# A two-layer recurrent block on one core: merged fp32r attention, paired output products, and experts routed through DRAM in 39 tiles

## The reference

```python
x = L0_attn_x                                  # [2, 1024, 256]
xn = layernorm(x)
q = rope(xn @ W_Q.T); k = rope(xn @ W_K.T); v = xn @ W_V.T   # 16 heads of 16, 8 key/value heads
s = softmax(q k^T / sqrt(256)) v  -> @ W_O.T
g = silu(swiglu(xn, lut[gate_idx], lut[up_idx], lut[down_idx]))      # inner width 688, 16-entry table
x = x + s * g
xn = layernorm(x)
s = time_mix(xn)        # layernorm again, w/k/v/r, state = (1-w) state + k v, y = r . state, @ Wout; 4 heads of 64
# experts: 8 of width 176, the best 2 of each token count; a shared one of width 352
combine = top-2 softmax weights, renormalised, zero for the other 6
out = silu(x @ shared_gate.T) * (x @ shared_up.T) @ shared_down.T
out = out + sum_e combine_e * (silu(x @ gate_e.T) * (x @ up_e.T)) @ down_e.T
x = x + s * silu(out)
```

## Time and profile before

| | us |
|---|---|
| median of 3 runs | 1142.14 (1138.51 to 1142.19) |
| profiled execution, first to last instruction | 1137.0 |
| outside that span (median less span) | 5.1 |

### The profile page before, as it was taken

One profiled execution on the slowest core, in us unless ns is written; L12 is line 12 of the kernel. 1 busy time (PEld: TensorE's weight loads), 2 busy tenths in 40 slices (PEclk: granted clock), 3 DMA queues, 4 the chain that ended last, 5 costly groups with the idle time before them and its releaser, 6 DMA issues. The chain is left out here.

```text
span 1137.0 us, 18228 instructions
## 1 busy us (share of the span) xinstructions
PE 1029.0 (91%) x7112; PEld 625.2 (55%) x7112; DVE 730.6 (64%) x993; ACT 489.1 (43%) x864; POOL 378.5 (33%) x304
## 2 busy tenths in 40 slices
PE   4869999999999999998999999846899999999997
PEld 3722333333333333322687878745756788888886
DVE  6889777778777877770376554499923574434433
ACT  1412666666556555656542244130621343332322
POOL 3231444346434543456011000296600042323232
PEclk9866999999999999999999999865599999999999
DMA  4580111111111111100200000230000111211211
GB/s 164 179 276 19 31 33 33 34 28 33 32 33 32 33 33 33 37 12 12 69 1 1 2 1 1 77 126 3 2 3 1 47 59 35 74 47 57 65 56 47
DMA packets 43606, 52.87 MB, mean 46 GB/s; under 512 B 14216, under 2 KB 30472, under 8 KB 43256
## 3 DMA queue, kind: packets, MB, share of 16 engines
q1 hardware_dynamic: 43104, 50.99, 14.4%
q10 hardware_dynamic: 416, 0.72, 0.2%
HBM read 37.53 MB, written 12.06 MB: 44 GB/s over the span
## 5 line engine op out<-in xcount | busy, mean ns | idle before, releaser
L626 DVE TENSOR_REDUCE row_max<-psum 128x1 f32<-128x1024 f32 x256 | 302.6, 1218 | 87.5 <-PE psum L679 87.4
L611 ACT ACTIVATE probs_t<-psum 128x512 f32<-128x512 f32 x512 | 267.1, 603 | 199.9 <-PE psum L693 199.9
L703 PE MATMUL psum<-probs_t,VS 128*32 128x512 f32 x1024 | 206.9, 604 | 17.5 <-ACT o_sb L494 17.5
L581 POOL TENSOR_TENSOR lut_sum<-lut_sum,lut_tmp 128x1072 f32<-128x1072 f32 x60 | 149.4, 2490 | 200.1 <-DVE lut_tmp L644 199.4
L679 PE MATMUL psum<-KS,QS 96*128 96x512 bf16 x512 | 164.6, 405 | 13.0 <-DVE row_max L626 8.9
L693 PE MATMUL psum<-QS,KS 99*128 99x512 bf16 x512 | 153.7, 381 | 3.2 <-ACT probs_t L611 3.2
L1858 POOL TENSOR_TENSOR m_h_f<-m_h_f,comb_b 128x512 f32<-128x512 f32 x44 | 71.5, 1625 | 234.0 <-DVE m_h_f L1936 234.0
L679 PEld LDWEIGHTS psum<-KS,QS 96*128 96x128 bf16 x512 | 39.0, 98 | 158.7 <-DVE row_max L626 114.6
L1936 DVE TENSOR_TENSOR m_h_f<-psum,m_silu 128x512 f32<-128x512 f32 x56 | 38.7, 691 | 124.9 <-ACT m_silu L1893 124.9
L693 PEld LDWEIGHTS psum<-QS,KS 99*128 99x128 bf16 x512 | 48.9, 97 | 99.9 <-ACT probs_t L611 49.9
L1893 ACT ACTIVATE m_silu<-psum 128x512 f32<-128x512 f32 x56 | 33.4, 597 | 154.7 <-PE psum L392 154.7
(11 more groups left out here) (228 smaller groups left out, 1729.4 us busy)
## 6 DMA issues: line engine op xcount, KB each, us to landing
QS<-q_rows SPq DMA_DIRECT2D x32, 192.0 KB
m_raw<-experts_w SPq DMA_DIRECT2D x2, 2688.0 KB, 13.0
comb_b<-comb_rows SPq DMA_DIRECT2D x16, 256.0 KB, 3.3
q_rows<-part SPq DMA_DIRECT2D x8, 384.0 KB, 3.1
KS<-k_rows SPq DMA_DIRECT2D x16, 192.0 KB
x_tok<-x SPq DMA_DIRECT2D x4, 512.0 KB, 7.9
q_rows<-part SPq DMA_DIRECT2D x8, 256.0 KB, 4.0
ctxT<-o_sb SPq DMA_DIRECT2D x64, 32.0 KB, 2.0
```

The costliest lines, as they stand in the source:

```text
L581: nc.gpsimd.tensor_tensor(wsum[:, cols], wsum[:, cols], wtmp[:, slot % 3, :], ALU.add).then_inc(lut_add, 1)
L611: nc.scalar.activation(pt[:, k % NPT, :], ring(k)[:], ACT.Exp, scale=float(E) ** -0.5).then_inc(p_ready, 1)
L626: nc.vector.tensor_reduce(mx[:, n % 2, i:i + 1], m.psum[:, 2 * (k % 2):2 * (k % 2) + 2, :], AX_XY, ALU.max).then_inc(max_done, 1)
L703: nc.tensor.matmul(OB[32 * j:32 * (j + 1), :], m.VS[:, bb * NTT + t, kv, :], pt[:, k % NPT, :], start=(t == 0), stop=(t == NTT - 1)).then_ ...
```

## The change

1. **Projections and attention become one block**; the semaphores of this front part are cleared after it, with a barrier. ACT now makes the normalised tiles (`scale`) in place of DVE, the parts are two (fp32r high and low) in place of three, so the DVE residue and the second ACT cut are gone, and the v projections of the last two token blocks stand among the first maxima.
2. **fp32r attention operands.** An operand is 48 rows (3 slots x 16), 50 with the maxima, held as fp32r. The two query heads of a group lie at rows 0 and 64. Each group's load is 768 KB (576 KB before), four groups are held (`NQK`), 26 maxima stand ahead of the first step. `place_max(0)` is issued ahead of the table-index loads.
3. **`output`** puts the two heads' A products side by side, then the two state products.
4. **Routing.** `route` runs two steps per slot, then 14 steps of `place` turn it into a row number for each token and choice, with counts made on PE (`count_tokens`). POOL scatters each token's row twice to `x_rows` in DRAM: 32 indirect DMAs of 128 rows. DVE waits for all of them before it takes `s_tok`.
5. **Experts.** Rows sorted by expert lie in 39 tiles of 128 rows; each is turned, goes through the one expert that its number (`tile_w`, loaded into a PE register) names, and is stored to `y_rows`. POOL gathers both results of each token (32 indirect DMAs), and DVE combines. On PE a place of the loop holds `gate_up` of tile i (6 matmuls of 352 columns), `turn_h` of i-1 (2 transposes), `down_r` of i-2 (6 matmuls of 256 columns) and `turn_x` of i+2 (2 transposes); ACT and DVE follow in the same order. SP loads tile j+1 behind the store of tile j-4. The shared expert (3 chunks) is dense over 4 blocks, the first before, three after the routed tiles.

The core of the diff:

```diff
@@ attention: PE
-    mm = nc.tensor.matmul(MX[k % 2][h][:], QS[n % 3][0:NROW, i * P:(i + 1) * P],
-                          KS[n % 3][0:NROW, h * BLK:(h + 1) * BLK], start=True, stop=True)
+    st, g = divmod(i, G)
+    mm = nc.tensor.matmul(MX[k % 2][h][:], QS[n % NQK][rows(g, NROW), st * P:(st + 1) * P],
+                          KS[n % NQK][rows(g, NROW), h * BLK:(h + 1) * BLK], start=True, stop=True)
...
-                    maxima_ahead(k)
+                    for h in range(2):
+                        maximum(k, h)
                     scores(n, t, 0)
+                    scores(n, t, 1)
                     if t >= 1:
                         weigh(n, t - 1)
                     elif n >= 1:
                         weigh(n - 1, NTT - 1)
-                    maxima_ahead(k + 1)
-                    for j in range(1, NJ):
-                        scores(n, t, j)
+                    scores(n, t, 2)
+                    scores(n, t, 3)
+                    for h in range(2):
+                        maximum(k + 1, h)
@@ time mix: POOL and DVE
+            pool.wait_ge(idx_done, NIDX)
+            for n in range(NT):
+                pool.wait_ge(m.xr_ready, n + 1)
+                for c in range(2):
+                    nc.gpsimd.indirect_dma_start(m.x_rows, bass.IndirectOffsetOnAxis(ap=m.slots[:, c, n:n + 1], axis=0),
+                                                 m.xr[:, n, :], None).then_inc(m.scat, 16)
...
+            dve.wait_ge(m.scat, 16 * 2 * NT)
             for n in range(0, NT, 2):
                 dve.wait_ge(so_ps, n // 2 + 1)
@@ experts: SP, the routed loop on PE, POOL
+            def load(j):
+                if j >= 4:
+
+                    sp.wait_ge(t1_ps, j - 3)
+                sp.dma_start(xs[:, j % 4, :], m.x_rows[j * P:(j + 1) * P, :]).then_inc(xs_in[j % 4], 16)
+
+            def store(j):
+                sp.wait_ge(yo_done, j + 1)
+                sp.dma_start(m.y_rows[j * P:(j + 1) * P, :], yo[:, j % 4, :]).then_inc(ys_out[j % 4], 16)
+
+            for j in range(NTL + 4):
+                if j < NTL:
+                    load(j)
+                if j >= 4:
+                    store(j - 4)
...
+            for i in range(-2, NTL + 2):
+                if 0 <= i < NTL:
+                    at_expert[i] = pe.value_load(m.tile_w[0:1, i:i + 1], min_val=0, max_val=(NE - 1) * EW)
+                    gate_up(i, at_expert[i])
+                if 0 <= i - 1 < NTL:
+                    turn_h(i - 1)
+                if 0 <= i - 2 < NTL:
+                    down_r(i - 2, at_expert[i - 2])
+                if 0 <= i + 2 < NTL:
+                    turn_x(i + 2)
...
+            for i in range(4):
+                pool.wait_ge(ys_out[i], 16 * len(range(i, NTL, 4)))
+            for tb in range(NB):
+                for n in range(tb * TPB, (tb + 1) * TPB):
+                    for c in range(2):
+                        nc.gpsimd.indirect_dma_start(y[:, c, n, :], None, m.y_rows,
+                                                     bass.IndirectOffsetOnAxis(ap=m.slots[:, c, n:n + 1], axis=0)
+                                                     ).then_inc(y_in[tb], 16)
```

More of the change, by code:

```diff
@@ new lines, in project_v @@
+    def project_v(pe, tb):
+        if tb >= 2:
+            pe.wait_ge(prod_q, 4 * NB)
+        pe.wait_ge(xt_lo, KC * (tb + 1))
+        for i in range(TPB):
+            tok = slice(tb * BLK + i * P, tb * BLK + (i + 1) * P)
+            mm = three(nc, bank[V_BANK[tb]][:, i * P:(i + 1) * P],
+                       [(m.xTh[:, kc, tok], m.xTl[:, kc, tok], wh[:, kc, 4 * P:], wl[:, kc, 4 * P:])
+                        for kc in range(KC)])
+        mm.then_inc(v_ps, 1)
+    m.project_v = project_v
@@ L441, in attention_stage @@
     mres_done = sem("mres_done")
-    AHEAD = NST // 2
+    AHEAD = 10
+    PAIRED = (2, 3, 0, 1)
     MX = [bank[0:2], bank[2:4]]
@@ L1449, in _ @@
             act.wait_ge(ad_put, 4 * NCH)
-            for i in range(2):
-                m.high_w(i)
+            act.wait_ge(idx_done, NIDX)
+            act.wait_ge(k_done, (NL - 1) * NCH)
+            nc.scalar.activation(m.wh[:, SHARED], m.raw[:, SHARED], ACT.Copy).then_inc(m.e_wh, 1)
         def low_y(dve, g):
@@ L1602, in _ @@
                     take_level(l, g)
-                    if (l - 2) * NCH + g < NSTEP:
-                        route((l - 2) * NCH + g)
+                    slot = (l - 2) * NCH + g
+                    for step in range(2 * slot, min(2 * slot + 2, NSTEP)):
+                        route(step)
+                    for step in range(2 * (slot - PLACE_AT), min(2 * (slot - PLACE_AT) + 2, NIDX)):
+                        if step >= 0:
+                            place(step)
             for g in range(NCH):
@@ L1788, in experts_stage @@
-    NX = sum(c < NEC for c in ORDER)
-    TURN_AT = 6
-    def ncomb(k):
-        return k // NMC * NX + sum(c < NEC for c in ORDER[:k % NMC + 1])
-    def slot(tb, i):
-        return place(tb, i) % 2 * 2
-    def place(tb, i):
-        return 1 + tb * (NMC + 1) + i + (i >= TURN_AT and tb < NB - 1)
-    def turn_place(g):
-        return 0 if g == 0 else 1 + (g - 1) * (NMC + 1) + TURN_AT
-    WHAT = {}
-    for tb in range(NB):
-        WHAT[turn_place(tb)] = ("x", tb)
-        for i in range(NMC):
-            WHAT[place(tb, i)] = ("h", tb * NMC + i)
@@ new lines, in experts_stage, with slot, wdn @@
+    (t1_ps, xth_done, xtl_done, gur_ps, silur_done, hr_done, t2_ps, hth_done, htl_done, dnr_ps, yo_done) = (
+        sem(n) for n in names)
+    xs_in = [sem(f"xs_in{i}") for i in range(4)]
+    ys_out = [sem(f"ys_out{i}") for i in range(4)]
+    y_in = [sem(f"y_in{i}") for i in range(NB)]
+    NQ = NSC + 1
+    SH = NE * EW
+    def slot(q):
+        return q % 2 * 2
+    def wgu(t, w, kc, c):
+        i = SH + (kc * 2 + w) * SI + SC[c][0]
+        return t[:, i:i + SC[c][1]]
+    def wdn(t, c):
+        i = SH + 2 * KC * SI + c * E
+        return t[0:SC[c][1], i:i + E]
@@ L1900, in _ @@
-            high(NB * NMC - 1)
-            gate_out(NB - 1)
+            for e in range(2):
+                high_w(e)
+            for c in range(NSC):
+                silu(0, c)
+                if c >= 1:
+                    high(0, c - 1)
+                high_w(2 + 2 * c)
+                high_w(3 + 2 * c)
+            high(0, NSC - 1)
+            keep_shared(0)
+            for i in range(-2, NTL + 2):
+                routed(i)
+            for tb in range(1, NB):
+                high_x(tb)
+                for c in range(NSC):
+                    silu(tb, c)
+                    if c >= 1:
+                        high(tb, c - 1)
+                high(tb, NSC - 1)
+                keep_shared(tb)
@@ L1948, in _ @@
-            low_h(NB * NMC - 1)
+            low_w(0)
+            for c in range(NSC):
+                product(0, c)
+                if c >= 1:
+                    low_h(0, c - 1)
+                low_w(2 + 2 * c)
+            low_h(0, NSC - 1)
+            dve.wait_ge(down_done, NSC)
+            nc.vector.memset(hr[:], 0.0).then_inc(hr_zero, 1)
+            for i in range(-2, NTL + 1):
+                routed(i)
+            m.once_normed(dve, 1)
+            for tb in range(1, NB):
+                low_x(tb)
+                if tb + 1 < NB:
+                    dve.wait_ge(t_ps, KC * (tb + 1))
+                    m.once_normed(dve, tb + 1)
+                for c in range(NSC):
+                    product(tb, c)
+                    if c >= 1:
+                        low_h(tb, c - 1)
+                low_h(tb, NSC - 1)
```

1099 lines of the change are left out of this document (654 added, 445 removed).

## The result

The changed kernel takes 1074.8 us (median of 4 runs, 1068.6 to 1079.4), the kernel before 1140.3 beside it: a ratio of 0.943, with a 95% interval of 0.939 to 0.947. The profiled execution has a span of 1072.4 us.

A forecast was written before the change was run, and what follows sets the result against it. Bound: a limit per stage, with PE-ACT latency in attention, DVE at the start and in levels, PE in experts. 1137.0 - 10 - 76 + 1.5 + 5 + 12 - 12 = 1057.5, plus 5.1 outside the span = 1062; range 1010 to 1116.

The forecast's parts named there:

- Start: Up to the first exponential: residues, normalising and a barrier leave VectorE, two maxima and v projections come back; -10 us.
- Steps: Attention steps: six matmuls cover the exponentials and row halves overlap; 2.95 us per step with maxima, 2.5 without; -76 us.
- Levels: Levels and routing: 14 place steps on VectorE at mean 0.35 us, counting matmuls hidden on TensorE; +5 us.
- Outputs and scatter: Time-mix outputs: paired products save 18 us on TensorE, but 32 indirect DMAs make the stage end later; +12 us.
- c: Scatter and gather: time of one indirect DMA on GpSimd, taken as 1.3 us, 32 each way.
- Experts: Expert stage: first block 20, routed tiles 141, shared blocks 50, tail 23, end 3; 237 us for 249.4, -12.
- my own loop: Routed tiles: result store, next load, turn_x and products form a wait loop over two tiles; T = 3.5 us per tile.
- Rival A: Routed loop runs at TensorE's 2.1 us per tile because loads land early enough; 55 us less, 1007; chance 0.13.
- B: Scatter: indirect DMAs are cheap, c = 0.5; 26 us less, 1036; chance 0.08.
- C: Scatter and gather: GpSimd held until each indirect DMA lands; 1140 at c = 2.8, 1172 at 3.3; chance 0.10.
- D: Attention steps: rows don't overlap and VectorE starves, 3.3 us per step; +44 us, 1106; chance 0.11.
- E: Routed tiles: T = 4.8 us with TensorE at the low clock between waits; +51 us, 1113; chance 0.10.

The follow-up runs named there:

- e_v: Changed kernel with the last two v projections split in eight parts and block 1's moved between two turns; first exponential at 103.2 us, was 103.0.
- d_half: Changed kernel with PAIRED (0, 1, 2, 3) for (2, 3, 0, 1), each score beside a maximum of its own row half; step 3.01 us for 2.79.
- b_zero: Changed kernel with GpSimd's zeroing of A held until VectorE's third placing step is done; levels 97.7 us, against 100.3 in three kernels at the same clock.
- c_unpair: Changed kernel with each head's state product behind its A product again in output; outputs 43.9 us for 24.9, s_tok 79.2 after the first output for 70.1.
- a_early: Changed kernel with SP storing tile j-6 instead of j-4 behind the load of tile j; 1039.4 us, ratio 0.910 to the kernel before.
- a_const: SP order of a_early plus a constant expert per tile, without register load or address arithmetic, against the changed kernel; 1040.6 us, routed tiles 99.9 us.
- f_weights: Changed kernel with the weight split of experts 4 to 7 moved before VectorE's wait for the scatter; s_tok to first routed tile 18.1 us for 27.8.
- b_bf16: Changed kernel with bf16 operands for the counting products in place of fp32; counting 1.1 us for 10.6, levels 95.3 us for 104.7.

## Why the prediction came out right, term by term

1062 was predicted, 1074.8 measured, inside 1010 to 1116. The span came out 14.9 above its term of 1057.5, and the time outside it 2.4 and not 5.1. (The 5.1 set a median beside the span of another execution; within one execution the kernel before takes 1.8 more than its span.) That the number came out so near is in part luck: the terms of the stages miss by 36 us in all, 25 us too low and 11 too high.

**Start: wrong, +2.7 for -10.** The four residues and the barrier went as said. Two terms failed. The end of the last rotation, put at 54.5, was at 59.6: VectorE waited 7.34 us for projections that TensorE made at clock 0.50 between 40 and 46. And the v projections, taken at 2 each out of 0.3 to 3, cost 5.24 each: 24 products at the low clock are 5.3 us (64.66 to 69.97) and the next maximum's own 1.2 more, and the buffered maximum covered 1.3 of them. `e_v` shows that neither was mine to win by moving these products: the operands' way through DRAM sets the first maximum, and after it TensorE at clock 0.50 and VectorE wait for each other, where I had VectorE's maxima alone as the bound.

**Steps: right in kind, 7 us better.** 2.79 a step for 2.95 while there are maxima; the jitter I added isn't there. `d_half` gave 3.01 without overlap against my 3.0. The 2.79 lies at VectorE's 2.8, but partly by chance, as relieving VectorE left 2.74. What I had wrong is the idea of a single bound: VectorE (96% busy) and TensorE's 2.65 lie so close that relief of one gains 0.05. The Trainium skill (TensorE: Matmul & The Clock Gate, Part 3: Packing small matmuls) lets products of distinct row groups run at once; the start times 0.01 apart agree, the price of 0.34 for a pair, where one takes 0.23, doesn't: half of the overlap is had. The 13 steps without maxima took 2.99 (44.8 / 15 with the two around them) and not 2.5, since the clock fell to 0.71; in `b_zero`, at 1.00, they took 2.39.

**Feed-forward and time-mix projections: +3.5 for +1.5.** No run looked into these 2 us.

**Levels: wrong, +12.9 for +5.** "The 31 counting matmuls hide on PE" was the step that failed, twice. The 32 products (two records each in fp32; the expectation above miscounts them as 47) take 10.6 us, and I put them against TensorE's idle time of the whole stage, while they stand in one piece ahead of two level products for which VectorE waits: 4.86 at the clock of the changed kernel, 0.85 at the full one. And a collision that I hadn't looked for: 5.3 us under GpSimd's zeroings, which the counting had bunched to three in a row. With bf16 counting 9.4 of the 12.9 go; what is left, 3.5, is no more than the 14 placing steps, which take 4.95 in all without the stalled time: 0.35 each, as taken. The Trainium skill (SBUF — State Buffer, Who interferes with whom) says that VectorE in its two-port modes and GpSimd exclude each other for a whole instruction. No row names the mode of the shift, but `b_zero` agrees, and adds that the loser may sit out three instructions in a row.

**Outputs and scatter: right, +14.8 for +12.** The pairs saved 19.0 for 18. c was taken as 1.3 and is 1.33 for the scatter (41.2 / 31) and 1.28 for the gather; 3 us more went into the half projection at the low clock and the first output. That VectorE's work beside the DMAs would push c up came true in one place above all, the 1.7 us of the long one shown with `c_unpair`. `c_unpair` shows the hiding, 9.9 us of it, where my sum had 9; the sentence in which I called all 18 hidden contradicts that sum, and the run.

**Experts: right in size, by errors that cancel.** Total -15.6 for -12. The routed tiles took 130.1 for 141, and the first block 27.7 for 20. The order of SP's list set the tile, as said: `a_early`. But within the tile the registers that I gave 1.2 cost 0 (`a_const`; so the 0.6 of the other estimate doesn't show either, which by my own loop would make 3.2 a tile and not 3.3), and TensorE's products take 2.46, not 2.1. With these two my loop gives (3.7 + 2.46) / 2 = 3.08, and half of the places took 3.13 or less: the mechanism was right, its products were mis-sized. Rival A's condition, loads that come in time, would have given 2.46 and not 2.1; its price was 30 us, not 55. The first block was long because VectorE's and GpSimd's differences held each other up (4.01 for 1.43); `f_weights` brings 18.1. The three shared blocks took 52.6 for 50, the tail 23.4 for 26.

Of the rivals, B, C, D and E did not come: c, the overlap and the tile were near what I took.

## What to carry to other kernels

An engine that issues loads and stores from one list in order couples them: issue a load before the store that waits for a later result. The order of SP's list was worth 30 us, nearly half of what the whole change brought. Work that fits an engine's idle share must also fit where it stands; ask who is queued behind it. And two engines whose chains are nearly equally long are both the bound: relief of one shows little, while work added to one of them shows soon (0.22 us a step in `d_half`).

## What the runs showed of the hardware

- A register load and ten register instructions in each tile on TensorE's sequencer cost nothing that can be measured beside 2.46 us of products (39 tiles in 99.9 us with and without).
- A 128x8 integer shift of VectorE took 5.30 us under three zeroings of GpSimd, 1.09 beside one (`b_bf16`) and 0.17 alone. It goes the other way too: an indirect DMA of GpSimd took 2.68 us beside a 128x2176 difference of VectorE, and 0.94 to 1.41 at most other times.
- Fp32 products of 8 columns took 0.18 us a record at a clock of 0.59; the 32 counting products took 7.3 us in fp32 at the full clock, 13.8 at half of it, and 1.1 in bf16 at the full clock.
- An indirect DMA of 128 rows of 1 KB takes GpSimd 0.96 us and comes every 1.26 to 1.36 us on the mean of 32.
- In all four kernels on one chip TensorE or ScalarE crawled for 20 to 40 us while GpSimd issued such DMAs, in none of the nine others. What that is stays open.
